# Router logits assembled from columns that ride with fc1 and fc2, and expert rows normalised on GpSimd

## What is computed

```
h = h + L1_attn(layernorm(h))      # neighbourhood attention
h = h + L1_ffn(layernorm(h))       # mixture of experts

L1_attn(x):  xs = x @ fc1_w.T + fc1_b;  ...;  return x + (xs @ fc2_w.T + fc2_b)

L1_ffn(x):   logits = x @ gate_w.T                 # 8 experts
             two largest of softmax(logits) -> weights w, slots in each expert (capacity 740)
             z = 2 * x;  z = z * rsqrt(mean(z * z) + 1e-6) * norm_w
             gu = z @ w13;  y = x + (silu(g) * u) @ w2
             out = sum over the two experts of w * y
```

## Time and profile before

| | us |
|---|---|
| median of 3 runs | 982.08 (981.37 to 984.68) |
| the profiled execution, its own time | 982.76 |
| its span, first to last instruction | 980.9 |
| PE busy | 858.5 (88%) |
| DVE busy | 455.5 (46%) |
| ACT busy | 318.1 (32%) |
| POOL busy | 280.1 (29%) |

### The profile page before, as it was taken

One profiled execution on the slowest core, in us unless ns is written; L12 is line 12 of the kernel. 1 busy time (PEld: TensorE's weight loads), 2 busy tenths in 40 slices (PEclk: granted clock), 3 DMA queues, 4 the chain that ended last, 5 costly groups with the idle time before them and its releaser, 6 DMA issues. The chain is left out here.

```text
span 980.9 us, 17879 instructions
## 1 busy us (share of the span) xinstructions
PE 858.5 (88%) x6209; PEld 621.5 (63%) x6209; DVE 455.5 (46%) x1520; ACT 318.1 (32%) x904; POOL 280.1 (29%) x242
## 2 busy tenths in 40 slices
PE   6899999899999999893997999977465999999991
PEld 6787888676466655463854777757453666666661
DVE  6864565548443322241654688836781222222220
ACT  2544333237433332240042566633101121221210
POOL 1540000000000000000233455530027488888444
PEclk9999999799899999996997899985556999999996
DMA  8992000270089999982500000002005354455222
GB/s 265 281 329 97 2 2 2 81 305 2 23 320 423 423 422 423 425 263 70 175 1 1 1 2 0 1 2 53 24 24 140 79 105 104 92 101 104 39 24 25
DMA packets 59881, 128.93 MB, mean 131 GB/s; under 512 B 26334, under 2 KB 42256, under 8 KB 50112
## 3 DMA queue, kind: packets, MB, share of 16 engines
q1 hardware_dynamic: 29858, 118.61, 33.3%
q0 software_dynamic: 29952, 9.36, 7.0%
HBM read 115.76 MB, written 11.49 MB: 130 GB/s over the span
## 5 line engine op out<-in xcount | busy, mean ns | idle before, releaser
L1831 POOL DMA_INDIRECT out_dram<-yr,put x48 | 105.7, 2203 | 58.3 <-issue 35.4
L1286 POOL MEMSET xg<- 96x74 f32 x1 | 0.2, 157 | 406.9 <-PE bank L1259 406.9
L1818 POOL DMA_INDIRECT zr<-z_rows,take x48 | 66.6, 1388 | 84.6 <-issue 84.6
L1895 PE MATMUL bank<-zTa,w 128*128 128x372 f32 x256 | 90.0, 496 | 0.8 <-DVE zTb L1969 0.8
L1978 DVE TENSOR_TENSOR hT<-sg,bank 128x372 f32<-128x372 f32 x64 | 31.8, 538 | 107.5 <-ACT sg L1939 63.1
L1895 PEld LDWEIGHTS bank<-zTa,w 128*128 128x128 f32 x256 | 47.5, 194 | 38.2 <-ACT sg L1939 8.4
L1143 DVE COPY eh<-bank 128x384 f32<-128x384 f32 x32 | 17.8, 558 | 110.6 <-PE bank L1181 110.6
L1909 PE MATMUL bank<-w2r,hT 128*124 128x192 f32 x384 | 66.1, 329 | 0.8 <-DVE hT L1978 0.8
L1939 ACT ACTIVATE sg<-bank 128x372 f32<-128x372 f32 x64 | 27.3, 478 | 115.4 <-PE bank L1900 115.4
L1909 PEld LDWEIGHTS bank<-w2r,hT 128*124 128x124 f32 x384 | 61.9, 187 | 3.8 <-issue 3.8
L1327 POOL TENSOR_TENSOR nl<-nl,nr 111x1036 f32<-111x1036 f32 x22 | 42.1, 1914 | 61.7 <-DVE nr L1437 61.7
(11 more groups left out here) (298 smaller groups left out, 1798.4 us busy)
## 6 DMA issues: line engine op xcount, KB each, us to landing
w1l<-in_w_dram SPq DMA_DIRECT2D x20, 1152.0 KB, 16.3
w2l<-in_w_dram SPq DMA_DIRECT2D x20, 1152.0 KB, 16.9
w1s<-in_w_dram SPq DMA_DIRECT2D x12, 1152.0 KB, 15.5
w2s<-in_w_dram SPq DMA_DIRECT2D x12, 1152.0 KB, 15.1
w<-in_w_dram SPq DMA_DIRECT2D x8, 1024.0 KB, 8.0
xt<-in_x_dram SPq DMA_DIRECT2D x22, 336.0 KB, 8.0
xT<-in_xT_dram SPq DMA_DIRECT2D x22, 333.0 KB, 7.4
w2r<-in_w2r_dram SPq DMA_DIRECT2D x8, 384.0 KB, 4.1
```

The lines of the kernel that those rows point to most:

```text
L1818: nc.gpsimd.indirect_dma_start(zr[b][:, j, :], None, z_rows, bass.IndirectOffsetOnAxis(ap=take[:, k:k + 1], axis=0), bounds_check=NROW - 1 ...
L1831: nc.gpsimd.indirect_dma_start(rows_out, bass.IndirectOffsetOnAxis(ap=put[:, k:k + 1], axis=0), yr[e % 2][:, j, :], None, bounds_check=OUT ...
L1895: nc.tensor.matmul(bank[to + 2 * part + half][:, 0:HS], w13[b][:, 0, at:at + 128], zTa[b][:, half * HS:(half + 1) * HS], start=True, stop= ...
```

## The change

- `fc1` gets eight more columns, the router's, so that bank 1 holds `xn @ gate_w.T` under the 96 rows of fc1's product. `fx` becomes one tile for all rows, [104, 2442], and its last eight rows keep those products. ACT copies eight rows of `fx` into the last eight rows of `nz` for each tile, ahead of its wait for `proj`.
- `fc2` becomes [104, 208]: sixteen columns stand ahead of the 192. The first eight hold `fc2_w.T @ gate_w.T` (made by PE and copied by ACT as the second half of near starts), the other eight pass the eight rows of `nz` through. Each tile's product thus leaves 16 numbers per row in bank 7 (the last two tiles in bank 1) at an offset that moves by 16 columns with the tile; `proj`, `nz` and `h` use the bank at that offset.
- As the second half of near starts, PE makes three small pairs of products (the router's columns by fc2's weights, by ones, and by `rbias`) behind the last key and ahead of the first value. `rbias` is made by two DVE operations ahead of near's norm constants. POOL makes `sd1` (the old deviation plus 1) and `lgc` once, behind the residual of tile 2.
- In route the loop over tiles is gone: no `hn`, no transposes, no copies, no router products. Between the variance and the reciprocal root DVE runs `parts`, seven operations that put the logits together, and after the root an eighth.
- `zk` is made by POOL, 22 operations ahead of its gathers, once `zs` is there (`s_ph`).

```diff
+            def parts():
+                dve.wait_ge(s_nb, 6)
+                early = bank[7][0:TP, 0:NLT * NLW].rearrange("p (t w) -> p t w", w=NLW)
+                late = bank[1][0:TP, 0:(T - NLT) * NLW].rearrange("p (t w) -> p t w", w=NLW)
+                both = ((early, 0, NLT), (late, NLT, T))
+                for k, (part, lo, hi) in enumerate(both):
+                    op = nc.vector.tensor_tensor(rlg[:, lo:hi], part[:, :, EX:NLW], sd1[:, lo:hi].unsqueeze(2).to_broadcast([TP, hi - lo, EX]), ALU.mult)
+                nc.vector.tensor_tensor(rlgm[:], per_row(hmean[:]), rsum[:, 0:EX].unsqueeze(1).to_broadcast([TP, T, EX]), ALU.mult).then_inc(s_r, 1)
+                dve.wait_ge(s_r, 1)
+                for part, lo, hi in both:
+                    nc.vector.tensor_tensor(rlg[:, lo:hi], rlg[:, lo:hi], part[:, :, 0:EX], ALU.add)
+                nc.vector.tensor_tensor(rlgm[:], lgc[:], rlgm[:], ALU.subtract).then_inc(s_r, 1)
+                dve.wait_ge(s_r, 2)
+                nc.vector.tensor_tensor(rlg[:], rlg[:], rlgm[:], ALU.add).then_inc(s_r, 1)
+
+            h_norm_constants(dve, 3, parts)
             dve.wait_ge(s_ln, 20)
+            dve.wait_ge(s_r, 3)
+            nc.vector.tensor_tensor(rlg[:], rlg[:], per_row(hrs[:]), ALU.mult).then_inc(s_r, 1)
...
-            def normalize(t, b):
-                if after(t, 2):
-                    dve.wait_ge(s_hTr, 5 * T // 2 + t - 1)
-                nc.vector.tensor_scalar(hn[b][:], h[:, t, :], hmean[:, bass.ds(t, 1)], hrs[:, bass.ds(t, 1)], ALU.subtract, ALU.mult).then_inc(s_hn, 1)
-                nc.vector.tensor_scalar(zk[:, t, :], h[:, t, :], hmean[:, bass.ds(t, 1)], zs[:, bass.ds(t, 1)], ALU.subtract, ALU.mult).then_inc(s_gz, 1)
-
-            over_tiles(dve, [(0, normalize)], T)
...
         def rows_pool(pool):
+            pool.wait_ge(s_ph, 9 + 4)
+            for t in range(T):
+                nc.gpsimd.tensor_scalar(zk[:, t, :], h[:, t, :], hmean[:, t:t + 1], zs[:, t:t + 1], ALU.subtract, ALU.mult).then_inc(s_gz, 1)
             pool.wait_ge(s_rt, 3)
...
             def proj(t, q):
                 b = q % 2
+                if after(t, 2):
+                    act.wait_ge(s_nF, t - 1)
+                nc.scalar.copy(nz[b][WN:WN + EX, :], fx[WN:WN + EX, bass.ds(t * TP, TP)])
                 act.wait_ge(s_nP, t + 1)
```

More of the change, by code:

```diff
@@ L66 @@
 PACK_D = [("phi", HALF, 2 * NE), ("scale", HALF, 1), ("image", TP, GB + 1), ("b1s", 128, NE * HB)]
[L68 to L71, removed]
+PACK_C = [("fc1", HALF, 2 * (WN + EX)), ("fc2w", HALF, 2 * WN), ("bfc2c", HALF, 2), ("conva", WN, CONV), ("convb", CONV, WN), ("wq", WN, WN), ("wk", WN, WN),
+          ("wv", WN, WN), ("proj", NHN * VW, WN), ("fc2", WN + EX, 2 * EX + ED), ("bv", TP, WN), ("bfc2", TP, ED),
+          ("bfc1", WN + EX, 1), ("bconva", CONV, 1), ("bconvb", WN, 1), ("bq", WN, 1), ("bk", WN, 1), ("bproj", WN, 1),
+          ("head", WN, NHN), ("before", TP, TP), ("count", TP, SP_), ("number", TP, T), ("spare", SP_, NST), ("real", TP, T),
           ("gain", 128, 2 * EX)]
@@ L297, in tower @@
         hpT = [sb(f"hpT{b}", [HALF, 2, PAIR]) for b in range(2)]
-        fx = [sb(f"fx{b}", [WN, PAIR]) for b in range(2)]
+        fx = sb("fx", [WN + EX, T * TP])
         fa = [sb(f"fa{b}", [CONV, PAIR]) for b in range(2)]
@@ L1273, in value_tiles, with router_columns, part_of @@
             return [t + 2]
+        def router_columns(c):
+            return Cc["fc1"][:, c * (WN + EX) + WN:(c + 1) * (WN + EX)]
+        def part_of(t):
+            if isinstance(t, int) and t >= NLT:
+                return bank[1], (t - NLT) * NLW
+            return bank[7], t * NLW
         def near_sp(sp):
@@ L1360, in near_dve @@
         def near_dve(dve):
+            dve.wait_ge(s_cci, 16)
+            for c in range(2):
+                nc.vector.tensor_scalar(rbias[:, c, :], router_columns(c), Cc["bfc2c"][:, c:c + 1], None, ALU.mult)
             h_norm_constants(dve, 2)
             dve.wait_ge(s_ln, 15)
-            dve.wait_ge(s_cci, 16)
             dve.wait_ge(s_pad, 1)
@@ L1375, in fc1 @@
                 dve.wait_ge(s_f1, p + 1)
[L1376 to L1379, removed]
+                nc.vector.tensor_scalar(fx[:, bass.ds(p * PAIR, PAIR)], bank[1][0:WN + EX, 0:PAIR], Cc["bfc1"], None, ALU.add).then_inc(s_f1c, 1)
             def convb(p, b):
@@ L1515, in fc1 @@
                 for c in range(2):
-                    last = nc.tensor.matmul(bank[1][0:WN, 0:PAIR], Cc["fc1"][:, c * WN:(c + 1) * WN], hpT[b][:, c, :], start=(c == 0), stop=(c == 1))
+                    last = nc.tensor.matmul(bank[1][0:WN + EX, 0:PAIR], Cc["fc1"][:, c * (WN + EX):(c + 1) * (WN + EX)], hpT[b][:, c, :], start=(c == 0), stop=(c == 1))
                 last.then_inc(s_f1, 1)
@@ L1539, in near_pe @@
             pe.wait_ge(s_hTc, 2 * T + T // 2)
+            for c in range(2):
+                nc.tensor.matmul(bank[6][0:WN, 0:EX], Cc["fc2w"][:, c * WN:(c + 1) * WN], router_columns(c), start=(c == 0), stop=(c == 1))
+            for c in range(2):
+                nc.tensor.matmul(bank[6][0:TP, EX:2 * EX], ones[0:HALF, 0:TP], router_columns(c), start=(c == 0), stop=(c == 1))
+            for c in range(2):
+                last = nc.tensor.matmul(bank[6][0:TP, 2 * EX:3 * EX], ones[0:HALF, 0:TP], rbias[:, c, :], start=(c == 0), stop=(c == 1))
+            last.then_inc(s_rw, 1)
             def query(t, q):
```

84 lines of the change are left out of this document (45 added, 39 removed).

## The result

The changed kernel takes 968.47 us (median of four executions, 962.73 to 971.18) where the kernel before took 982.10 beside it: a ratio of 0.985, interval 0.981 to 0.989. 967 was predicted, with 962 to 976 as the range. The profiled execution took 967.93 us, its span is 965.4.

What follows compares the result with a forecast made beforehand. Route was taken as bound by a chain of single steps, PE's turns of transposes and router products at half clock; -21.7 + 1.7 + 0.7 + 0.2 + 0.2 + 4.0 = -14.9 us gave 967 us, range 962 to 976.

Steps and rivals of the forecast that it cites:

- Term 1: Route, `hmean` to `top`: removing the loop over tiles leaves 4.8 us instead of 26.5, 21.7 us less.
- Term 2: Start of near's second half: three pairs of small PE products between last key and first value, 1.7 us more.
- Term 3: Near's loop: wider `fc2` 0.7 us more, ACT's copies 0.2 more, `rbias` ahead of `hmean` 0.2 more.
- Term 4: Route's search and prefix sums: `zk` on POOL makes DVE's steps wait, 4 us more from `top` to the gather.
- light contention: Search beside POOL: only forms like `hp` wait, costing 0 to 2 us; time 963 to 965, chance 0.27.
- the forecast's case: Search beside POOL: contention of 2 to 8 us, time 965 to 971, chance 0.55.
- the 2.9 us counted up to `hots`: Search up to `hots`: ten of fourteen DVE steps wait for POOL, together 2.9 us.
- the 1.1 in the prefix sums: Prefix sums after the search: the last six or so POOL operations meet them, half free, 1.1 us more.
- the six steps: Search steps following another of their kind, each waiting nearly one POOL operation of 0.42 us.
- the rival of late rows: First gather: waits for POOL's `zk` rows if one operation needs over 1.5 us; at 3 us about 996; chance 0.04.
- The signs to look for: Profile after: listed marks such as `top` about 5 us behind `hmean` and 41 us from `top` to the gather.

Runs made afterwards that it cites:

- before_zk_pool: The kernel before with only `zk` moved from DVE to POOL, the loop over tiles staying: 984.18 us, ratio 1.000 to the kernel before.
- products_first: The changed kernel with the six small products moved ahead of near's first transposes, replacing three filling products: 963.82 us, ratio 0.978 to the kernel before.
- zk_act: The changed kernel with the 22 `zk` normalisations on ACT, POOL making only their offsets: 963.12 us, ratio 0.980 to the kernel before.
- zk_twice: The changed kernel with POOL making all 22 `zk` twice, only the second round releasing the rows: 985.15 us, ratio 1.002 to the kernel before.

## Why the prediction was right, and where it was not

- **Term 1 held.** The loop was worth 22.2 us, 21.7 were predicted. The steps between `hmean` and `top` come as worked out, and nothing took the loop's place. `before_zk_pool` shows that PE, and not DVE's `zk`, had set the loop's pace.
- **Term 2 was too small by half a microsecond**: 2.2 instead of 1.7. It was sized by the router's product, 0.57 us for a pair; a pair of these takes 0.72 from start to start. That they stand on the path was right, and `products_first` gives back all they cost.
- **Term 3 held in sum**: 0.7 from the first value to the last `fc2` (0.9 predicted). Its parts were off: the wider `fc2` costs about 0.3, not 0.7; the copies about 0.4, not 0.2 (both from one trace without the copies). The 0.2 of `rbias` can't be told from the start's scatter.
- **Term 4 is the step that failed.** 4 us were predicted, with light contention as a rival at 0 to 2; it is 1.7 to 1.9, and `zk_act` shows that POOL is the cause of it. By its size that is the rival (0.27), not the forecast's case (2 to 8 us, 0.55); but the rival's condition, that forms like `hp` wait, doesn't hold either. The failing sentence is "The nearest row is `hp` (SBUF in, SBUF out, not a reduction), so I let them wait". That row was of another POOL operation, and even `hp`'s form hardly waits beside `zk` (`before_zk_pool`). Of nine search steps of 176 columns with two inputs in SBUF, seven kept 0.33 to 0.36 us. So of the 2.9 us counted up to `hots` 0.3 came (`top` to `sums` takes 6.86 us, 6.54 before), of the 1.1 in the prefix sums 0.9 (`sums` to the first mark 7.77, 6.90 before), and 0.5 came where none was counted: the slots start 0.2 later behind the marks and last 0.3 longer. Before, the first mark stood here:

```profile
705.40 0.36 DVE L1772 TENSOR_TENSOR oht<-cc,col 111x192 f32<-111x192 f32 x1
```

- **Two errors of term 4 worked against each other.** It took 0.42 us for a POOL operation, and one took 1.03. Had the six steps waited as it says, the right price would have made them 6 x 0.61 = 3.7 us dearer, and the term nearly 8 instead of 4 (an estimate). That the term came out only 2.3 too large is luck.
- The Trainium skill's rule on which term 4 leaned (SBUF — State Buffer, Who interferes with whom: a two-input DVE instruction and a GpSimd instruction that reads SBUF exclude each other) fits the first `eq`, 0.52, and the last `hots`, 0.45, and not the seven others. By the same section copies and one-input forms can contend too. The small copies of the prefix sums agree, 0.17 to 0.23 us before and 0.26 to 0.39 after; `hn` hardly does, with 0.40 in the median beside `zk` instead of 0.38.
- **`zk`'s price was outside its bounds.** 0.27 to 0.59 us was taken from a copy and a two-input add; it is 1.00 to 1.78. It did no harm because the rows had time to spare, but 9 us instead of 20. With the right price the rival of late rows would have deserved more than 0.04: its threshold of 1.5 us a tile stood only 0.3 above the mean of 1.18 (25.98 by 22). `zk_twice` shows that rival as it was described.
- **The total was closer than its terms.** With a contention of 1.7 and small products of 2.2, the same sum gives about 965.5 us, the edge of the rival of light contention (963 to 965). The first comparison came out at 968.47, with near's `hmean` 2.7 us late in its profiled execution; when the same kernel ran again the median was 963.34, and over both sets of four executions it is 966.3. So 967 was met with a contention that is 2.3 us too large and a start that scatters by more than that; that it was met within 1.5 us is in part luck. The 3 us (0.3%) that the prediction gave a measurement are too few: the eight executions of the changed kernel lie 10 us apart.
- **The signs to look for.** As said: `top` 5 us behind `hmean`, seven operations between `hvar` and the root, no DMA at the gather, the slots at half clock. Not so: the gather stands 38.9 us behind `top`, neither 41 nor the 37 that would have refuted term 4; the two-input steps of the search mostly keep 0.34 us and don't go to 0.8; `zk` takes 1.0 us and more, not 0.3 to 0.6; the three pairs of products take 2.15 us, not 1.7.

What stays open: why `hp` waits out POOL's adds, of 384 columns as of 1036, and `hn` hardly waits for POOL's `zk`. The adds have two inputs and `zk` one with two scalars per partition; no run varies that alone. Open is also what decides which search steps are stretched.

## What to carry to other kernels

A stall seen under one operation of a neighbouring engine is no price for another operation there: size contention by a row with the same pair, or carry both ends as cases of equal weight. Before work is moved to an idle engine, ask which idle engine does it cheapest and shares least with the path: ACT did in 0.53 us, and for nothing, what POOL did in 1.0 and at 1.9 us of the search. When a loop goes, read what the next stretch is bound by: here it was PE at 1.2 GHz in the slots (granted clock 0.50), and keeping PE busy up to their start and in them was worth 3.4 us, and 5.1 with `zk` on ACT.

## What the runs showed of the hardware that was not expected

- A GpSimd operation with one input tile and two scalars per partition (111x192) takes 1.00 us, longer than its add of two tiles of the same size, 0.59; the same work takes 0.53 us on ACT, and on DVE one follows the other after 0.29.
- Beside DVE's search POOL kept 1.03 us an operation while DVE kept 0.34 for most two-input steps. Beside the marks it was POOL that lost: its operations took 1.45 us in the mean and 1.78 at most.
- The same DVE form waits out one POOL operation and hardly another of the same length: `hp` took 1.05 us beside an add of two inputs that took 1.06, `hn` 0.40 in the median beside `zk` of 1.03.
- PE busy for 20.01 of 20.39 us in the slots stayed at a granted clock of 0.50 for their whole length; with one product of 256 columns ahead of each pair, and PE busy up to their start, the clock was 1.00 throughout.
- The start of the program, up to near, scatters by 10 us from one execution to the next (473.97 to 484.08), with median landing times of the input tile `xt` of 7.5 to 9.4 us. That is more than most parts of this change are worth.
